# One pipeline per token tile for mix, gate and main products, and low-rank products moved between the linear products

## The reference, cut to what matters

```python
y = einsum('bct,bcd->bdt', x, cond_w[cond])            # mix
h = relu(layernorm(y @ gw1.T + gb1)); gates = h @ gw2.T + gb2
top_v, top_i = top_k(gates, 2); g = softmax(top_v)
allowed = counts_of(top_i) <= capacity                 # needs all tokens
w = sum_k(onehot(top_i) * g * allowed)
x1 = x + y @ weight.T + ((y @ lora_A) * w) @ lora_B / 16
z = x1 @ w1[adapter].T                                 # linear, per batch
out = x1 + bitlinear((bitlinear(z, w_gate) * bitlinear(z, w_up)), w_down)
# bitlinear: scale = mean(|w|), w -> round(clip(w / scale, -1, 1)) * scale
```

## Time and profile before

| | us |
|---|---|
| median of 3 runs | 1432.23 (1428.03 to 1435.14) |
| span of the profiled execution | 1483.3 |

### The profile page before, as it was taken

One profiled execution on the slowest core, in us unless ns is written; L12 is line 12 of the kernel. 1 busy time (PEld: TensorE's weight loads), 2 busy tenths in 40 slices (PEclk: granted clock), 3 DMA queues, 4 the chain that ended last, 5 costly groups with the idle time before them and its releaser, 6 DMA issues.

```text
span 1483.3 us, 24909 instructions
## 1 busy us (share of the span) xinstructions
PE 1350.7 (91%) x8870; PEld 861.8 (58%) x8871; DVE 744.4 (50%) x1102; ACT 367.0 (25%) x404; POOL 141.8 (10%) x79
## 2 busy tenths in 40 slices
PE   5778898999845999799999999999999999999998
PEld 4775444444422454354554468884488864788843
DVE  5457555432341443488886635558155564355531
ACT  3231343100100113477773101111011120011100
POOL 3200000000000000000000002320012220022200
PEclk8889899999977999899999999999999999999999
DMA  8993599759999491699996464335554444643354
GB/s 215 269 258 114 187 398 417 252 164 232 173 240 170 163 248 43 237 328 334 326 310 231 177 239 149 148 139 201 184 181 154 153 174 170 214 149 148 139 213 135
DMA packets 174492, 310.62 MB, mean 209 GB/s; under 512 B 99520, under 2 KB 131520, under 8 KB 166624
## 3 DMA queue, kind: packets, MB, share of 16 engines
q1 hardware_dynamic: 159232, 254.23, 55.3%
q10 hardware_dynamic: 14176, 55.06, 10.9%
q0 software_dynamic: 1024, 0.53, 0.2%
HBM read 220.78 MB, written 68.03 MB: 195 GB/s over the span
## 4 chain that ended last, share of the span: by engine, by line
PE 55%; DMA 19%; DVE 8%; SPq 6%; issue 5%; ACT 5%; POOL 0%; ACTq 0%; POOLq 0%; DVEq 0%
PE pair L934 25%; PE pair L971 13%; PE pair L795 8%; DMA region_w<-w1s_scratch 6%; PE pair L730 4%; DMA region_q<-in_L_cond_weight 3%; SPq L493 3%; DMA region_q<-in_x 3%; DMA wb_scratch<-region_q 3%; DMA region_q<-wb_scratch 3%; ACT region_q L1149 2%; PE pair L639 1%; DVE region_q L1597 1%; DMA region_w<-in_L_ffn_w_gate 1%; ACT region_q L1165 1%
## 5 line engine op out<-in xcount | busy, mean ns | idle before, releaser
L934 PE MATMUL pair<-act_t,region_q 128*128 128x256 f16 x3696 | 404.0, 273 | 0.0
L934 PEld LDWEIGHTS pair<-act_t,region_q 128*128 128x128 f16 x3696 | 361.6, 98 | 42.5
L971 PE MATMUL pair<-region_q,region_w 128*128 128x512 f16 x1232 | 267.8, 379 | 4.5 <-DMA region_q<-wb_scratch 4.2
L624 POOL TENSOR_TENSOR region_w<-region_q,region_w 128x1792 f32 (+1 forms) x33 | 118.4, 3586 | 1245.9 <-ACT region_w L1174 1245.9
L795 PE MATMUL pair<-region_w,act_t 128*128 x816 | 182.0, 384 | 48.7 <-DMA region_w<-w1s_scratch 47.4
L971 PEld LDWEIGHTS pair<-region_q,region_w 128*128 128x128 f16 x1232 | 120.0, 98 | 151.0 <-DMA region_q<-wb_scratch 6.3
L730 PE MATMUL pair<-region_w,act_t 128*128 128x512 f16 x768 | 171.2, 380 | 0.0
L795 PEld LDWEIGHTS pair<-region_w,act_t 128*128 x816 | 80.5, 99 | 144.5 <-issue 54.2
L898 PE MATMUL pair<-act_t,region_q 128*128 128x512 f16 x704 | 158.1, 384 | 0.0
L1288 DVE SCALAR_TENSOR_TENSOR act_t<-pair,act_t 128x512 f32 (+2 forms) x66 | 61.1, 947 | 135.7 <-ACT act_t L1004 135.7
L730 PEld LDWEIGHTS pair<-region_w,act_t 128*128 (+1 forms) x768 | 75.4, 98 | 87.5 <-issue 0.8
(11 more groups left out here) (185 smaller groups left out, 1035.7 us busy)
## 6 DMA issues: line engine op xcount, KB each, us to landing
region_q<-wa_scratch SPq DMA_DIRECT2D x33, 1792.0 KB, 7.3
region_q<-wb_scratch SPq DMA_DIRECT2D x28, 1408.0 KB, 6.0
region_q<-in_L_cond_weight SPq DMA_DIRECT2D x40, 512.0 KB, 9.6
w1s_scratch<-region_q ACTq DMA_DIRECT2D x40, 512.0 KB, 8.5
wa_scratch<-region_q SPq DMA_DIRECT2D x22, 896.0 KB, 5.7
region_q<-in_x SPq DMA_DIRECT2D x64, 256.0 KB, 8.0
region_w<-in_L_ffn_w_gate SPq DMA_DIRECT2D x16, 688.0 KB, 12.2
wb_scratch<-region_q SPq DMA_DIRECT2D x11, 896.0 KB, 4.1
```

Source lines behind the costliest of these rows:

```text
L624: pool.tensor_tensor(at(iop[:, 1], u), st[s][:, 0:7], at(iop[:, 0], u), ALU.subtract)\
L934: mm = pe.matmul(bank(s_bank, b)[:, (1 - h) * HALF:(2 - h) * HALF], ring_a[s][:, h, o_a, k], moving[a], start=(opens and h == 1 and k == 0 ...
L971: mm = pe.matmul(bank(s_bank, b), iop[:, a, p, o_a, tp * P:(tp + 1) * P], ring_b[r][:, p], start=(opens and p == 0 and a == 0), stop=(not ...
```

## The change

Mix, gate and main products run in one loop over t: mix(t), gate(t - 1), main(t - 3), all unrolled. PSUM pair 0 holds mix, pair 1 gate, pairs 2 and 3 the main products. `main_part` (DVE) adds x from its buffer (six buffers, so x is loaded once) and writes the sum over the used columns of `act_t`, as f32. All five adapters are prepared in the turns t = 2 to 11, one `w_step` of four blocks a turn; w_gate pieces are loaded and summed two a turn for t = 4 to 11, by ACT (Abs with accumulation) and no longer by DVE. The gate arithmetic is done in quarters of four tiles (t = 6, 9, 13, 16), the counts and weights after the last. w0 has eight buffers, half of them loaded by ACT. Rank 0 is loaded as soon as all mixes, three quarters and all w_gate sums are done. After the last main product the low-rank products get PSUM groups of their own; `x1_sum` (DVE) adds them to the kept sum. Lora products and `turn_x1` stand in and between the linear products by the tables TURNS and LORAS; x1 has three buffers. The linear products up to the 13th are unrolled for it.

```diff
+LAG = 3
+NXR = 6
+NX1 = 3
+NSG = 3
+QT = NT // 4
+WLAG = 2
+GATES_AT = {3: (0,), 4: (1, 2), 5: (3, 4), 6: (5,), **{t: (t - 1,) for t in range(7, NT + 1)}}
+LAST_TURN = 12
+QUARTER_AT = {6: 0, 9: 1, 13: 2, 16: 3}
+SUMS_AT = {t: (2 * t - 8, 2 * t - 7) for t in range(4, 12)}
+TURNS = {**{k: (k + 1,) for k in range(4)}, 4: (5, 6), 5: (7,), 6: (8,), 7: (9,), 8: (10, 11), 9: (12,), 10: (13,),
+         11: (14,), 12: (15,)}
+LORAS = {**{k: (k + 2,) for k in range(3)}, 3: (5, 6), 4: (7,), 5: (8,), 6: (9,), 7: (10, 11), 8: (12,), 9: (13,),
+         10: (14,), 11: (15,), 12: ()}
...
+            def load_x(t):
+                slot = t % NXR
+                wait_if(sp, acc_released, t - NXR + 1)
                 b0 = field(sp, F_PERM, 2 * t, NB - 1)
                 b1 = field(sp, F_PERM, 2 * t + 1, NB - 1)
...
+                sp.dma_start(x_nat[slot][0:SEQ, :], x_rows[ds(b0 * SEQ, SEQ), :]).then_inc(x_loaded[slot], 16)
+                sp.dma_start(x_nat[slot][SEQ:P, :], x_rows[ds(b1 * SEQ, SEQ), :]).then_inc(x_loaded[slot], 16)
...
+            def load_w(row_i, j):
+                for q in range(4):
+                    if j == 0:
+                        sp.wait_ge(w0_transposed, q + 1)
+                    else:
+                        sp.wait_ge(w_low, 4 * j + q - 3)
+                    sp.dma_start(w_nat[q], w1_rows[ds(row_i + (4 * (j % 2) + q) * P, P), :]).then_inc(w_loaded[q], 16)
...
+            def load_gate(p):
+                s = p % NSG
+                if p < NSG:
+                    sp.wait_ge(ag_high, 3)
+                    sp.wait_ge(ag_low, 3)
+                wait_if(sp, gate_summed, p - NSG + 1)
+                sp.dma_start(stat_gate[s], gate_flat[:, p * PIECE_G:(p + 1) * PIECE_G]).then_inc(gate_loaded[s], 16)
...
+            for t in range(WLAG, NT + WLAG):
+                if t + 2 < NT:
+                    load_x(t + 2)
+                j = t - WLAG
+                row_i = field(sp, F_ADP, j // 2, NADP - 1) * D
+                if j < 2:
+                    load_w(row_i, j)
+                else:
+                    with sp.If(used > j // 2):
+                        load_w(row_i, j)
+                for p in SUMS_AT.get(t + 1, ()):
+                    load_gate(p)
...
+            sp.wait_ge(y_done, NT)
+            sp.wait_ge(quarter_done, 3)
+            sp.wait_ge(gate_summed, NPIECE_G)
+            for s in range(4):
+                sp.wait_ge(w_stored[s], stores(0))
             load_rank(0)
             sp.wait_ge(main_done, NT)
...
+            for t in range(NT + LAG - 1):
+                if t < NT:
+                    mix(t)
+                early = GATES_AT.get(t, ())
+                if t <= 3:
+                    if t == LAG:
+                        main(0)
+                    for g in early:
+                        gate(g)
+                    continue
+                gate(early[0]) if early else None
+                main(t - LAG)
+                for g in early[1:]:
+                    gate(g)
+                if t == NT:
+                    pe.wait_ge(count_ready, 1)
+                    pe.wait_ge(tmp_copied, NT)
+                    pe.matmul(pair[1][:, 0:2 * E], ones[:, :], cnt[:, :, :].rearrange("p a b -> p (a b)"),
+                              start=True, stop=True).then_inc(counted, 1)
+
...
+            def lora(t):
+                if t == 0:
+                    pe.wait_ge(tmpw_low, 2)
+                elif t == 2:
+                    pe.wait_ge(acc_released, NT)
+                elif t > 2:
+                    pe.wait_ge(x1_ready, t)
...
+            main(NT - 1, (0, 1, 2))
+            lora(0)
+            main(NT - 1, (3,))
+            turn_x1(0)
+            lora(1)
...
+            for k in range(LAST_TURN + 1):
+                turns, loras = TURNS[k], LORAS[k]
+                linear(k, k % 2, {4: turns[0]} if len(turns) == 1 else {3: turns[0], 6: turns[1]},
+                       {6: loras[0]} if len(loras) == 2 else {})
+                if loras:
+                    lora(loras[-1])
+                if k > 0:
+                    linear_t(k - 1, (k - 1) % 2)
...
+            def sum_gate(p):
+                s = p % NSG
+                act.wait_ge(gate_loaded[s], 16 * (p // NSG + 1))
+                act.activation(stat_gate[s], stat_gate[s], ACT.Abs, accum_out=stat_g[:, p:p + 1])\
+                   .then_inc(gate_summed, 1)
...
+            def main_part(t):
+                slot = t % NXR
+                v.wait_ge(main_done, t + 1)
+                v.wait_ge(tmp_done, t + 1)
+                v.scalar_tensor_tensor(out=x1p(t), in0=rows_of(pair[2 + t % 2][:, :]), scalar=1.0 / PROD,
+                                       in1=rows_of(x_nat[slot]), op0=ALU.mult, op1=ALU.add).then_inc(acc_released, 1)
...
+            def x1_sum(t):
+                v.wait_ge(lora_done, t + 1)
+                if t >= NX1:
+                    v.wait_ge(x1_transposed, t - NX1 + 1)
+                    v.wait_ge(x1_stored[t % NX1], 16 * (t // NX1))
+                acc = pair[t if t < 2 else 3]
+                v.scalar_tensor_tensor(out=rows_of(x1_nat[t % NX1]), in0=rows_of(acc[:, :]), scalar=1.0 / PROD,
+                                       in1=x1p(t), op0=ALU.mult, op1=ALU.add).then_inc(x1_ready, 1)
...
```

More of the change, by code:

```diff
@@ L245, in build_program @@
         gate_half = sem("gate_half")
+        quarter_done = sem("quarter_done")
         var_ready = sem("var_ready")
@@ L734, in lora, with main @@
-            def lora(t, s):
+            def main(t, quarters=range(4)):
+                acc = pair[2 + t % 2]
+                for q in quarters:
+                    if q == 0:
+                        pe.wait_ge(y_low, t + 1)
+                        wait_if(pe, acc_released, t - 1)
+                        if t < 2:
+                            pe.wait_ge(w0_low, KC)
+                    for k in (2 * q, 2 * q + 1):
+                        for a, b in ((0, 0), (0, 1), (1, 0)):
+                            for h in range(2):
+                                mm = pe.matmul(acc[:, h * H:(h + 1) * H], act_t[:, a, k, t * P:(t + 1) * P],
+                                               w0_t[:, 4 * h:4 * h + 4, b, k, :],
+                                               start=(k == 0 and a + b == 0), stop=(k == KC - 1 and a == 1))
+                    if q == 3:
+                        mm.then_inc(main_done, 1)
@@ L1016, in _ @@
                  WGT_SCALE).then_inc(ag_high, 1)
-            for r in range(2, NPREP0):
+            for r in range(2, KC):
                 high_w0(r)
+            for t in range(2):
+                y_part(t)
             act.wait_ge(lora_loaded, 16 * (KC + 1))
@@ L1064, in _ @@
-            act.activation(row[:, 2, :], row[:, 1, :], ACT.Sqrt).then_inc(gate_std, 1)
-            act.wait_ge(gap_ready, 1)
-            act.activation(row[:, 5, :], row[:, 4, :], ACT.Exp).then_inc(gate_exp, 1)
+            used = field(act, F_USED, 0, NADP)
+            for t in range(WLAG, NT + WLAG):
+                if t < NT:
+                    y_part(t)
+                if t == NT:
+                    tmp_part(NT - 1)
+                if t in QUARTER_AT:
+                    gate_root(QUARTER_AT[t])
+                if t == NT:
+                    act.wait_ge(gap_ready, 1)
+                    act.activation(row[:, 5, :], row[:, 4, :], ACT.Exp).then_inc(gate_exp, 1)
+                j = t - WLAG
+                if j < 2:
+                    w_step(j)
+                else:
+                    with act.If(used > j // 2):
+                        w_step(j)
+                if t < NT:
+                    for g in GATES_AT.get(t, ()):
+                        tmp_part(g)
+                for p in SUMS_AT.get(t, ()):
+                    sum_gate(p)
@@ L1527, in _ @@
-            with v.Fori(1, NT // 4) as i:
-                layer0(i, False)
-            with v.Fori(NT // 4, NT // 2) as i:
-                layer0(i, True)
-            low_x1(NT - 1)
+            x1_sum(0)
+            main_part(NT - 1)
+            low_x1(0)
+            x1_sum(1)
             v.wait_ge(gate_summed, NPIECE_G)
```

661 lines of the change are left out of this document (275 added, 386 removed).

## The result

| | us |
|---|---|
| kernel before, median of 4 runs | 1433.68 (1428.03 to 1446.01) |
| kernel after, median of 4 runs | 1486.65 (1463.23 to 1503.04) |
| after / before | 1.0254, 95% interval 1.0128 to 1.0380 |
| span of the profiled execution after | 1461.6 (that run took 1463.23) |

What follows compares the result with a forecast made beforehand. The kernel was taken as PE-bound, except a mix and gate stage waiting for DMA and one hole at 463 us. Linear product at 280 instead of 346 saves 66, less 33.3 moved: 1432.2 - 33 = 1399 us, range 1367 to 1427.

Steps and rivals of the forecast that it cites:

- The company of the turns: Turns 4 to 11: x tile, half a w1 adapter and two w_gate pieces each, so 17.5 us a turn against PE's 14.0.
- seven such rounds and a remainder: Main stage: seven rounds of 17.5 us to ACT's first sum of turn 11 at 191.0, then turn 13 at 194.9.
- The 2.0 us of excess a w_gate piece: Turns 4 to 11: a gate piece in flight costs 2.0 us more than its bytes at 417 GB/s.
- the SP chain through ACT's sum: Turns: SP's second gate piece load waits for ACT's sum, next x and w1 loads queue behind; a round takes 17.4 us.
- the wait for the counts: After turn 16: PE waits for DVE's last gate quarter, 13.5 us under a 10.4 us main product; 3 us bare.
- the 30.3 of moved products: Linear stage: 14 lora products of 1.29 us and 14 more x1 turns of 0.87 move in, all on PE.
- the x1 chain: Linear stage: x1_low late where two turns share one product (k = 4, 8), 1 to 2 us each, 3 in all.
- the 33 us gained: Up to and through the linear stage, without rank waits: 346 - 280 = 66, less 33.3, leaves 33 us saved.
- The waits for ranks: Linear products waiting for transposing loads: 47.4 us becomes 16 in the profiled run; taken as absent from unprofiled runs.
- The fourth: Rival, linear stage: x1 chain in ACT's queue behind piece loads; at 4 us a turn 1451 us; chance 0.08.
- The first: Rival, linear stage: rank waits are in the median too, giving 1368 us, or 1384 with half; chance 0.18.
- hole before the seventh product: Sign, linear stage: a wait before the seventh linear product; rank 2's load, 53.8 us, leaves 13 us bare.

Runs made afterwards that it cites:

- a_nog: Kernel after with only 16 columns of each w_gate piece loaded: 1497.43 us, ratio 1.0417 to the kernel before.
- a_spord: Kernel after with SP issuing the two w_gate pieces of a turn one turn later: 1490.43 us, ratio 1.0388 to the kernel before.
- a_nop: Kernel after with only 16 columns of each w_up and w_down piece loaded: 1440.27 us, ratio 1.0038 to the kernel before.
- b0: Kernel before run again, differing only by a blank line: 1431.71 us, ratio 1.0002; profiled span 1429.6 us.
- b_xst: Kernel before with 12 more x1 tile stores on ACT's queue, one after each linear product: 1497.85 us, ratio 1.0481.
- c1: Kernel after with w_gate pieces issued a turn later and w_up and w_down pieces in turns 12 to 17: 1469.64 us, ratio 1.0255 to the kernel before.
- b_xld: Kernel before with 12 more x tile loads of 0.52 MB on ACT's queue, one after each linear product: 1487.46 us, ratio 1.0424.
- a_pool: Kernel after with the x1 stores issued by POOL (GpSimd) instead of ACT: 1486.31 us, ratio 1.0206 to the kernel before.
- a_nox1s: Kernel after with only 16 columns of each x1 tile stored and the final residual read from x: 1440.88 us, ratio 1.0070 to the kernel before.

## Why the prediction was wrong

- **The company of the turns.** That PE needs 14.0 us and something else paces the turn was right, and the length of a turn nearly, 17.5 against 18.5. The sum, though, put only seven such rounds and a remainder between the start of turn 5 (66.6) and turn 13 (194.9), 128.3 us; measured 73.33 to 221.09, 147.8. That 17.5 came close is luck, since its reason was wrong in two points. The 2.0 us of excess a w_gate piece, from one window of 6 us, aren't there: a_nog. And the SP chain through ACT's sum is real (75.8 us in seven waits) but only one of two, and worth 0.8 us a turn by itself (a_spord, 17.7): the prediction named what stands behind that wait, and not that the w1 loads also stand behind the x tile's wait for `main_part`. Both SP orders mended: 16.1. Of the terms without a row, SP's issue was put at 0.8 us and takes 4.3 from the x load to the end of the four w1 loads (a_spord, 179.57 to 183.90). PE needed more than 14.0 as well, 121.9 us busy in the eight turns: the four mixes behind the longest waits took 2.7 to 3.4 us instead of 2.0, at a granted clock of 0.93 over the stretch. The fixed 2.0 us plus bytes over 436 GB/s that the prediction quotes is in the Trainium skill ("DMA: Bandwidth & Descriptors", "Anatomy of one DMA") a fit for transfers issued by GpSimd, and those here are issued by SP and ACT; the sum doesn't use it.
- **The rest of the way to the first linear product.** Turn 5 began 6.7 us late (3.6 of it already at the first mix, 27.56 instead of 23.95). From turn 13 to the first linear product 85.4 us against 85.1 forecast; the wait for the counts was 0.9 instead of 3, and turning tmp 1.75 instead of the estimated 3. In all 306.5 instead of 280.
- **The linear stage.** a_nop's stage is 43.7 us longer than b0's. PE is busy 32.9 us more in it, near the 30.3 of moved products, and idle 10.8 more, where the sum had 3 for the x1 chain. In a_nop's waits of PE x1 turns that wait for `low_x1` make 6.1 us in four waits (two of 2.2 in the products with two turns), lora products that wait for `x1_sum` 1.0, and seven small ones put down to "issue" 4.7, of which b0 has 1.2.
- **Without rank waits**, then, the 33 us gained are 9 lost at `gate_up` (559.95 against 550.98) and some 5 in the median: 26.5 from the turns and the front, 10.4 from the linear stage, and 4.8 because before reaches its first linear product at 341.2 in an ordinary execution and not at 346 (and 4.4 of b0's 341.2 are its one rank wait).
- **The waits for ranks: the step that failed in sign.** The inference that they are absent from before's median was right (b0: 4.4 us). From this I took that they would be absent after too, and carried the 33 us alone. But the trace of before held the warning: it showed that the loads can collapse (74.8 us for rank 2 beside pieces), and the change adds 14 stores of 0.52 MB to just that stretch. The sum has no term for those stores and names no reason for leaving them out; for the waits of ranks 1 and 2 it counted pieces alone. b_xst shows the price of such transfers in before, 68 us; taking them out of after takes it from 1474.56 to 1440.88. So the forecast had nothing where after has 34 us by the medians. The 22.2 us that the prediction read as a rank alone run from the first issue to the last landing of two loads; the bytes of an undisturbed load move at 290 GB/s (b0, a_nop), so the 261 GB/s that it quoted from the Trainium skill was nearer than it said.
- **The rivals.** The fourth had the sign (slower through something new in the linear stage) and another mechanism; at 0.08 it was priced as a chain of queues of 52 us, of which 10.8 came. The first, that rank waits are in the median too and would shrink, was true for after in its first half and false in its second.
- **The signs named.** Mixes 17.5 apart and SP waiting for ACT's Abs line: seen, at 18.5. Linear products 13.4 apart: in after the first nine steps average 15.2, seven of them 12.5 to 15.3 and the two others 19.4 and 18.4, where two turns share a product. The sign of being wrong, products waiting for `low_x1`, was seen too: 7.0 us in five waits. No hole before the seventh product; in after's profile it stood before that of the last rank.

The spread was a sign too, and free: a_nop runs within 1.4 us, after within 40. A time that swings between executions of one kernel points to something that depends on how transfers happen to meet.

## What to carry to other kernels

List for each stretch which streams run at once, and ask of every transfer that a change adds not whether it is hidden but whom it meets; a DMA transpose is the one to keep alone: beside one other stream it slowed at times (before, c1), beside two it did in both profiles of before with a third stream, and all eight executions of b_xst and b_xld took 1476 us or more. On an in-order issue queue put the loads whose buffers are free ahead of the load whose buffer isn't. A long execution of the kernel before, one in eight here, isn't noise to subtract: it shows which mechanism a change can make common.

## What the runs showed of the hardware

- A transposing load's packets of 256 bytes took 18 to 21 ns of an engine each, alone or in turn with pieces (b0, a_nop), 55 ns beside pieces in a slowed stretch (before, c1), and 147 ns in the hole of b_xst: 7 times as long. Ordinary transfers slow as well: in after's slowed stretch an x1 store took 24.1 us and a load of 0.94 MB 37.4.
- DMA's busy share doesn't give its rate: 1.25 stood beside 109 GB/s in b_xst, 1.03 beside 417 in before.
- It takes no store: loads do the same (b_xld). It isn't a matter of one queue (a_pool). It takes no third stream, which only makes it frequent.
- It wants bytes under way, not many transfers: with 16 columns of each, the same number of them does no harm (a_nop, a_nox1s). The Trainium skill ("DMA: Bandwidth & Descriptors", "Queues, rings and completion order") has each engine go round its queues packet by packet; that by itself explains neither the taking of turns in b0 nor a slowdown of all at once. Why two or three transfers take turns in one execution and crawl in the next stays open, and why b_xst suffers more than after does.
